# Each context group directly behind the scores of an even step, in a fused FFN, attention and FFN layer

## The chip, the core and the metric

The kernel runs on one core of a Trainium2 chip. Its time is the device time in microseconds (us) from launch to end; three runs of the kernel before took 852.42, 853.59 and 855.54 us, the median is 853.59 us. The core has TensorE (PE in the rows; PEld are its weight loads), VectorE (DVE), ScalarE (ACT), GpSimd (POOL) and SyncE (SP, which only issues DMAs here). Each engine works through its own instructions in order; they are held together by semaphores.

## The reference

The input x has 32 sequences of 256 tokens with 128 features (8192 tokens), float32. Three blocks follow one another:

```
x = x + 0.5 * ffn(layernorm(x))
x = x + attention(layernorm(x))
x = x + 0.5 * ffn(layernorm(x))

ffn(x):        h = concat([x, -x]);  h = 2*relu(s0 * h @ sign(k0));  h = 2*relu(s1 * h @ sign(k1))
               return s2 * h @ sign(k2)                 # 256 -> 512 -> 512 -> 128, weights +1 or -1
attention(x):  Q, K, V = x @ W.T + b, 16 heads of 8 features
               ctx = softmax(Q K^T / sqrt(8)) V         # per head, 256 x 256
               return layernorm(ctx + x) * gamma + beta
```

## The kernel before, in words

**Tiles and iterations.** A tile is 512 tokens, two sequences (b = 0, 1), so there are 16 tiles. `steps(it)` is written once for each engine and runs for iterations 0 to 16. An iteration has 32 steps (`UNITS`), and in it the stages of neighbouring tiles are interleaved by hand: the attention of tile t begins in step 0 of iteration t, its first FFN was done in the iteration before, the second half of its softmax falls into the first half of iteration t+1, and its second FFN later. Iterations 2 to 13 are the regular loop (`full`, L234). Iterations 0, 14 and 15 place the FFN pieces by tables of their own (`PACE_ZERO`, `PACE_FIRST`, `PACE_SECOND`, L44), iteration 1 has no FFN in its first half, and iteration 16 is the drain, with context places of its own (`AT_CONTEXT_LAST`).

**Attention.** 16 pairs p of a tile are two heads' scores for one sequence. In each even step `lanes` (L661) issues on TensorE the scores of pair s/2 into `ps_s` (L645) and, eight pairs behind, the shifted scores of another pair into `ps_t` (L658). VectorE takes row maxima of `ps_s` (`row_maxima`, L1049, the instruction of L1055). Scores wait until the maximum of the pair before is taken (`s_max`), shifted scores until the exponential of the pair before is taken (`s_exp`), since each has one buffer. ScalarE takes the exponential of `ps_t` into `probs` (`exps`, L824). The maxima of four pairs are split by GpSimd (L471 to L474), transposed by TensorE into the upper half of `ps_c` (`max_transpose`, L712, in steps 10, 17, 25 and 2), copied by ScalarE (`copy_max`, L833, in the step behind each: 11, 18, 26 and 3) and placed by a DMA as extra rows of Q, with which the shifted scores come out less their maximum.

**Context.** A context group is two pairs (four lanes): 16 float32 matmuls of 32 columns by 256 into the lower half of `ps_c` (`context`, L682, L698). There are eight groups a tile, C0 to C7. A group waits for the exponentials of its two pairs, and an even-numbered group (g % 2 == 0) also for the last copy out of `ps_c` (`c_free`) and for the maxima's copy (`mt_free`):

```
pe.wait_ge(s_exp, 2 * n + 2)
if g % 2 == 0:
    at_least(pe, c_free, GROUPS * t + grp // 2)
    ...
    pe.wait_ge(mt_free, 4 * t + (min(4, 2 + grp // 2) if last_tile else 2 + grp // 2))
```

Behind an odd-numbered group ScalarE copies the result to `ctx_t` (`context_copy`, L838, L841). Two of these, transposed by TensorE (`context_transpose`, steps 4 and 18, named CT0 and CT1), are divided by the softmax sums on VectorE and go to the tail on GpSimd (L477 to L499).

**FFN.** An FFN is 16 pieces (`ffn_piece`, L588). Piece 0 is the transpose of the normed input, pieces 2 to 5 the first layer (`ffn_in`, L560, L561), 6 to 11 the second (`ffn_mid`, L570, L571), 12 to 14 the last (`ffn_out`, L581, L583). Each result of 128 x 512 in one of the two banks `ps_z` is split in a high and a low float16 part: the high one by ScalarE (`z_split`, L798), then the low one by VectorE (`z_rest`, L1005, issued one step later), which frees the bank (`z_free`). In the regular loop the second FFN of a tile has pieces 2 to 14 in steps 2 to 14, the first FFN of a later tile in steps 18 to 30. Piece 0 stands in steps 15 and 31, and steps 0, 1, 16 and 17 have no FFN matmul.

**The order in a step.** On TensorE: `lanes` (in even steps), the context group if the step has one, the FFN piece, then the transposes and projections of the step (LNT 9, Q 12, K 15, V 31). On ScalarE: the exponentials, the FFN's split, the maxima's copy, the context's copy, the splits of the projections. On VectorE: the FFN rest of the step before, the row maxima, then norms, tail and projections.

Of the kernel before, what the change touches and what calls it, by code (L numbers as in the profile page):

```python
# [19 lines left out]
GROUPS, LANES = 4, 4  # L20
# [7 lines left out]
HALF = 16  # L28
# [59 lines left out]
def macaron_layer(nc, x, wq, bq, wk, bk, wv, bv, gamma, beta, k0, k1, k2, s0, s1, s2, out):  # L88
# [5 lines left out]
    with ExitStack() as ctx:  # L94
# [214 lines left out]
        def contexts(it, s):  # L309

            if not it.cur:
                return it.t - 1, 1 - it.par, (AT_CONTEXT_LAST.index(s) + 3,) if s in AT_CONTEXT_LAST else ()
            if s <= HALF + 1:
                return it.t - 1, 1 - it.par, (s // LANES + 3,) if it.prev and s % LANES == 1 else ()
            return it.t, it.par, ((s - HALF - 5) // LANES,) if s in (21, 25, 29) else ()

        def pair_of(p):

# [227 lines left out]
        def _(pe):  # L546
# [210 lines left out]
            def steps(it):  # L757
                t, par = it.t, it.par
                for s in range(UNITS):
                    lanes(it, s)  # L760
                    tile, parity, groups = contexts(it, s)
                    for g in groups:
                        context(tile, parity, g)
                    for f, _, piece in ffn_work(it, s):
                        ffn_piece(f, piece)
                    if it.prev:
                        if s == (AT_MAX[3] if it.cur else 1):
                            max_transpose(t - 1, 3)
                        for b in range(2):
                            if s == at(it, f"CT{b}"):  # L770
                                context_transpose(t - 1, b, it.misc[f"CT{b}"])
                    if it.cur:
                        for hb in range(3):
                            if s == AT_MAX[hb]:
                                max_transpose(t, hb)
                    if it.prep:
                        if s == at(it, "LNT"):
                            att_transpose(t + 1, 1 - par, it.misc["LNT"])
                        if s == at(it, "Q"):
                            project(0, it.misc["Q"])  # L780
                        if s == at(it, "K"):
                            project(1, it.misc["K"])
                        if s == at(it, "V"):
                            project_v(it.misc["V"])
# [7 lines left out]
        def _(act):  # L792
# [79 lines left out]
            def steps(it):  # L872
                t, par = it.t, it.par
                for s in range(UNITS):
                    tile, _, pairs = softmax_pairs(it, s)
                    for p in pairs:
                        exps(tile, p)
                    for f, _, piece in ffn_work(it, s):
                        ffn_piece(f, piece)

                    if it.prev and s - 1 == (AT_MAX[3] if it.cur else 1):
                        copy_max(t - 1, 3)
                    if it.cur and s - 1 in AT_MAX[:3]:
                        copy_max(t, AT_MAX.index(s - 1))
                    tile, _, groups = contexts(it, s)
                    for g in groups:
                        context_copy(tile, g)
                    if it.prep:
                        if s == at(it, "LNT"):
                            att_split(it.misc["LNT"])  # L890
                        if s == at(it, "Q"):
                            qk_split(0, it.misc["Q"])
                        if s == at(it, "K"):
                            qk_split(1, it.misc["K"])
                        if s == at(it, "V"):
                            v_copy(t + 1, 1 - par, it.misc["V"])
# [309 lines left out]
```

## Time and profile before

| | |
|---|---|
| median of three runs | 853.59 us |
| the profiled execution | 853.7 us |
| its span, first to last instruction | 851.9 us |
| TensorE busy, matmuls | 721.5 us (85%), 7258 matmuls |
| VectorE busy | 643.5 us (76%) |
| ScalarE busy | 513.3 us (60%) |
| GpSimd busy | 375.6 us (44%) |
| context matmuls (L698) | 2048, busy 139.6 us, idle before them 0.0 us |
| scores (L645) | 1024, busy 102.4 us, idle before them 39.0 us |
| row maxima (L1055) | 256, busy 312.4 us, 1220 ns each |
| mean granted clock of TensorE | 0.967 |

"Busy" is the time in which an engine has an instruction running; matmuls overlap in the pipeline, so a row's duration is longer than the distance to the next one. "Idle before" is the time in which an engine stood still just ahead of instructions of a row, with the instruction that ended it. A clock of 1.00 is TensorE's full speed, 2.4 GHz; 0.50 is 1.2 GHz.

### The profile page before, as it was taken

The numbers are of one execution on the slowest core, as the hardware profiler recorded it, in microseconds if no ns is written. First come the engines' busy times: TensorE is split into PE (matmuls) and PEld (weight loads), VectorE is DVE, ScalarE is ACT, GpSimd is POOL, SyncE is SP. The second block draws the span as 40 slices with busy tenths as digits, with TensorE's granted clock in tenths as the row PEclk, the third lists the DMA queues.
The fourth block names the chain that finished last, engine by engine and source line by source line (L and its number), as shares of the span: only waits on it lengthen the run. The fifth ranks groups of instructions, "written<-read, shape, count | busy, mean of one in ns | idle before, by whom it ended". The sixth has DMA issues, their size and how long they took to land. (4 is left out here: it accounts for less than half of the span.)

```text
span 851.9 us, 18411 instructions
## 1 busy us (share of the span) xinstructions
PE 721.5 (85%) x7258; PEld 325.4 (38%) x7258; DVE 643.5 (76%) x1228; ACT 513.3 (60%) x739; POOL 375.6 (44%) x663
## 2 busy tenths in 40 slices
PE   6768688899998988899998888899998987977666
PEld 2433234444443434444443334344443333332333
DVE  6558778878787888878787888878787887767343
ACT  3326566766666666766666666666666666656532
POOL 4522453536355353536355453536445453435240
PEclk9989899999999999999999999999999999989797
DMA  3101010101101010101101010100101010100000
GB/s 65 38 19 45 14 45 14 58 15 40 33 4 56 15 57 15 58 14 39 33 2 58 14 58 15 57 15 32 40 3 57 14 58 3 45 15 2 15 13 12
DMA packets 29508, 25.62 MB, mean 30 GB/s; under 512 B 4336, under 2 KB 29424, under 8 KB 29424
## 3 DMA queue, kind: packets, MB, share of 16 engines
q1 hardware_dynamic: 28992, 24.07, 9.1%
q8 instruction: 58, 0.95, 0.5%
q10 hardware_dynamic: 432, 0.39, 0.1%
q14 instruction: 26, 0.21, 0.1%
HBM read 5.05 MB, written 4.19 MB: 11 GB/s over the span
## 5 line engine op out<-in xcount | busy, mean ns | idle before, releaser
L1055 DVE TENSOR_REDUCE row_max<-ps_s 128x4 f32<-128x1024 f32 x256 | 312.4, 1220 | 89.8 <-PE ps_s L645 89.5
L830 ACT ACTIVATE probs<-ps_t,score_scale 128x1024 f32<-128x1024 f32 x256 | 283.9, 1109 | 122.8 <-PE ps_t L658 121.3
L798 ACT ACTIVATE ffn_hi<-ps_z 128x512 f16<-128x512 f32 x288 | 168.9, 592 | 139.0 <-PE ps_z L571 76.2
L1005 DVE SCALAR_TENSOR_TENSOR ffn_lo<-ps_z,ffn_hi 128x512 f16<-128x512 f32 x256 | 174.5, 686 | 74.8 <-ACT ffn_hi L798 71.9
L570 PE MATMUL ps_z<-ffn_hi,w 128*128 128x512 f16 x512 | 196.4, 384 | 5.9 <-DVE ffn_lo L1005 5.9
L571 PE MATMUL ps_z<-ffn_lo,w 128*128 128x512 f16 x512 | 194.9, 381 | 0.0
L698 PE MATMUL ps_c<-probs,v_cols 128*32 128x256 f32 x2048 | 139.6, 391 | 0.0
L645 PE MATMUL ps_s<-k_rows,q_rows 32*128 32x256 f16 x1024 | 102.4, 278 | 39.0 <-DVE row_max L1055 31.0
L658 PE MATMUL ps_t<-q_rows,k_rows 32*128 32x256 f16 x1024 | 102.2, 278 | 4.5 <-ACT probs L830 4.5
L471 POOL TENSOR_TENSOR max_scaled<-row_max,max_unit 128x16 f32<-128x16 f32 x64 | 14.2, 222 | 176.1 <-DVE row_max L1055 176.1
L570 PEld LDWEIGHTS ps_z<-ffn_hi,w 128*128 128x128 f16 x512 | 49.9, 98 | 88.4 <-issue 24.0
L698 PEld LDWEIGHTS ps_c<-probs,v_cols 128*32 128x32 f32 x2048 | 54.0, 110 | 61.3 <-issue 29.3
L645 PEld LDWEIGHTS ps_s<-k_rows,q_rows 32*128 32x128 f16 x1024 | 29.7, 92 | 123.8 <-DVE row_max L1055 87.8
L581 PE MATMUL ps_z<-w,ffn_hi 128*128 128x128 f16 x512 | 69.7, 224 | 3.9 <-DVE ffn_lo L1005 3.7
L560 PE MATMUL ps_z<-ffn_hi,w 128*128 128x512 f16 x128 | 51.6, 403 | 24.6 <-DVE ffn_lo L1005 20.2
L583 PE MATMUL ps_z<-w,ffn_lo 128*128 128x128 f16 x512 | 69.0, 223 | 0.0
L571 PEld LDWEIGHTS ps_z<-ffn_lo,w 128*128 128x128 f16 x512 | 50.3, 98 | 43.5 <-issue 1.0
L581 PEld LDWEIGHTS ps_z<-w,ffn_hi 128*128 128x128 f16 x512 | 48.8, 99 | 28.9 <-issue 20.4
L450 POOL TENSOR_TENSOR tail_ve<-tail_mv,eps 128x2 f32<-128x2 f32 x32 | 6.2, 195 | 114.5 <-DVE tail_mv L988 114.5
L583 PEld LDWEIGHTS ps_z<-w,ffn_lo 128*128 128x128 f16 x512 | 51.1, 100 | 0.3
L561 PE MATMUL ps_z<-ffn_lo,w 128*128 128x512 f16 x128 | 50.6, 395 | 0.0
L481 POOL TENSOR_TENSOR att_y<-ctx_n,xn_bv 128x256 f32<-128x256 f32 x32 | 23.3, 727 | 39.1 <-DVE ctx_n L1068 39.1
(119 smaller groups left out, 965.0 us busy)
## 6 DMA issues: line engine op xcount, KB each, us to landing
x<-L_attn_x SPq DMA_DIRECT2D x16, 256.0 KB, 2.7
q_rows<-q_hi SPq DMA_DIRECT2D x32, 128.0 KB, 2.1
y<-x SPq DMA_DIRECT2D x16, 256.0 KB, 2.1
k_rows<-k_hi SPq DMA_DIRECT2D x30, 128.0 KB, 2.1
q_rows<-q_lo SPq DMA_DIRECT2D x16, 128.0 KB, 2.1
q_rows<-no_max SPq DMA_DIRECT2D x16, 128.0 KB, 2.1
k_rows<-k_lo SPq DMA_DIRECT2D x15, 128.0 KB, 2.1
q_rows<-max_rows SPq DMA_DIRECT2D x64, 8.0 KB
```

The costliest lines, as they stand in the source:

```text
L560: pe.matmul(o[:], w0[:, m * P:(m + 1) * P], ffn_hi[:, 0, :], start=True, stop=False)
L570: pe.matmul(o[:], w, ffn_hi[:, 1 + k, :], start=(k == 0), stop=False)
L571: last = pe.matmul(o[:], w, ffn_lo[:, 1 + k, :], start=False, stop=(k == KC - 1))
L581: pe.matmul(o, ffn_hi[:, 5 + k, i * P:(i + 1) * P], w2[:, k, :], start=(i == 0 and k == 0), stop=False)
L583: last = pe.matmul(o, ffn_lo[:, 5 + k, i * P:(i + 1) * P], w2[:, k, :], start=False, stop=(i == TT - 1 and k == KC - 1))
L645: return pe.matmul(ps_s[:, i, a * SEQ:(a + 1) * SEQ], q_rows[par][r, g, c:c + P], k_rows[par][r, g, b * SEQ:(b + 1) * SEQ], start=True, st ...
L658: return pe.matmul(ps_t[:, i, a * SEQ:(a + 1) * SEQ], k_rows[par][r, g, c:c + P], q_rows[par][r, g, b * SEQ:(b + 1) * SEQ], start=True, st ...
L698: last = pe.matmul(ps_c[ROWS * j:ROWS * (j + 1), 0:SEQ], v[:, col:col + ROWS], probs[grp % 2][:, j, a * SEQ:(a + 1) * SEQ], start=(a == 0 ...
L798: a_.activation(ffn_hi[:, use, :], ps_z[use % 2][:], ACT.Relu if use else ACT.Copy, scale=1.0 if use else XN_SCALE).then_inc(z_hi, 1)
L830: a_.activation(probs[grp % 2][:, j:j + 2, :], ps_t[:], ACT.Exp, scale=score_scale[:, 0:1]).then_inc(s_exp, 1)
L1005: v.scalar_tensor_tensor(out=ffn_lo[:, use, :], in0=ps_z[use % 2][:], scalar=0.0, in1=ffn_hi[:, use, :], op0=ALU.max, op1=ALU.subtract).th ...
L1055: v.tensor_reduce(row_max[hb % 2][:].rearrange("p (a l) e -> p l a e", a=2)[:, j:j + 2, :, g % 2], ps_s[:].rearrange("p l (a k) -> p l a k ...
```

## The change

Only the helper `contexts(it, s)` is changed, which tells TensorE (matmuls) and ScalarE (copy) which context group stands in a step. In an iteration with current work the groups of the tile before stood in steps 1, 5, 9, 13 and 17 (C3 to C7) and those of the current tile in 21, 25 and 29 (C0 to C2). They now stand in steps 0, 4, 8, 12, 16 and 20, 24, 28. In these even steps the group comes directly behind `lanes` and ahead of the FFN piece and of the transposes and projections of the step. The drain (iteration 16) is as before, and so is every other instruction.

```diff
             if not it.cur:
                 return it.t - 1, 1 - it.par, (AT_CONTEXT_LAST.index(s) + 3,) if s in AT_CONTEXT_LAST else ()
-            if s <= HALF + 1:
-                return it.t - 1, 1 - it.par, (s // LANES + 3,) if it.prev and s % LANES == 1 else ()
-            return it.t, it.par, ((s - HALF - 5) // LANES,) if s in (21, 25, 29) else ()
+            if s <= HALF:
+                return it.t - 1, 1 - it.par, (s // LANES + 3,) if it.prev and s % LANES == 0 else ()
+            return it.t, it.par, ((s - HALF - LANES) // LANES,) if s in (20, 24, 28) else ()
```

`HALF` is 16, `LANES` is 4.

## Rows read from the trace of the kernel before

**Rows 1.** The header of the profile's page.
```profile
span 851.9 us, 18411 instructions
```

**Rows 2.** Windows: stretch and length; busy us (instructions) of PE, PEld, DVE, ACT, POOL; clock; DMA.
```profile
100.00:106.00 6.00, 4.42 (x30) 1.62 (x34) 3.62 (x7) 3.07 (x4) 4.26 (x6) 0.50 0.01 1
200.00:400.00 200.00, 180.74 (x1911) 82.40 (x1909) 164.78 (x312) 132.20 (x192) 96.07 (x171) 1.00 0.10 32
```

**Rows 3.** TensorE's timeline (start, duration, idle before): first scores of iterations 2 and 13.
```profile
134.41 0.28 PE L645 MATMUL ps_s<-k_rows,q_rows 32*128 32x256 f16 x2
...
662.81 0.28 PE L645 MATMUL ps_s<-k_rows,q_rows 32*128 32x256 f16 x2
```

**Rows 4.** TensorE's timeline, iteration 8, steps 4 to 8.
```profile
425.93 0.28 PE L645 MATMUL ps_s<-k_rows,q_rows 32*128 32x256 f16 x2
...
427.06 0.39 PE L560 MATMUL ps_z<-ffn_hi,w 128*128 128x512 f16 x1 [0.72 <-DVE ffn_lo L1005]
...
428.03 1.07 PE L698 MATMUL ps_c<-probs,v_cols 128*32 128x256 f32 x16
429.03 0.39 PE L560 MATMUL ps_z<-ffn_hi,w 128*128 128x512 f16 x1
...
432.18 0.28 PE L645 MATMUL ps_s<-k_rows,q_rows 32*128 32x256 f16 x2 [0.39 <-DVE row_max L1055]
```

**Rows 5.** ScalarE's timeline, iteration 8, steps 3 and 5.
```profile
426.64 0.36 ACT L836 ACTIVATE max_rows<-ps_c 16x256 f16<-16x256 f16 x1
...
429.67 0.60 ACT L798 ACTIVATE ffn_hi<-ps_z 128x512 f16<-128x512 f32 x1 [1.20 <-PE ps_z L561]
```

**Rows 6.** VectorE's timeline, iteration 8, steps 5 and 6.
```profile
428.64 0.68 DVE L1005 SCALAR_TENSOR_TENSOR ffn_lo<-ps_z,ffn_hi 128x512 f16<-128x512 f32 x1
...
430.30 0.69 DVE L1005 SCALAR_TENSOR_TENSOR ffn_lo<-ps_z,ffn_hi 128x512 f16<-128x512 f32 x1 [0.25 <-ACT ffn_hi L798]
430.91 1.22 DVE L1055 TENSOR_REDUCE row_max<-ps_s 128x4 f32<-128x1024 f32 x1
```

**Rows 7.** TensorE's timeline, iteration 8, steps 12 to 16.
```profile
440.36 0.28 PE L645 MATMUL ps_s<-k_rows,q_rows 32*128 32x256 f16 x2
...
440.69 0.23 PE L581 MATMUL ps_z<-w,ffn_hi 128*128 128x128 f16 x1
...
441.59 0.38 PE L619 MATMUL ps_m<-att_hi,wt_hi 128*128 128x512 f16 x1
...
442.55 1.07 PE L698 MATMUL ps_c<-probs,v_cols 128*32 128x256 f32 x16
...
444.11 0.28 PE L645 MATMUL ps_s<-k_rows,q_rows 32*128 32x256 f16 x2
...
446.30 0.28 PE L645 MATMUL ps_s<-k_rows,q_rows 32*128 32x256 f16 x2
```

**Rows 8.** ScalarE's timeline, iteration 8, steps 11 and 12.
```profile
440.96 0.36 ACT L836 ACTIVATE max_rows<-ps_c 16x256 f16<-16x256 f16 x1
...
442.66 0.69 ACT L815 ACTIVATE q_hi<-ps_m,b_fit 128x512 f16<-128x512 f32 x1 [0.34 <-PE ps_m L619]
```

**Rows 9.** VectorE's timeline, iteration 8, steps 13 and 14.
```profile
443.51 0.72 DVE L1046 SCALAR_TENSOR_TENSOR q_lo<-ps_m,b_fit,q_hi 128x512 f16<-128x512 f32 x1
444.54 1.23 DVE L1055 TENSOR_REDUCE row_max<-ps_s 128x4 f32<-128x1024 f32 x1 [0.31 <-PE ps_s L645]
```

**Rows 10.** TensorE's timeline, iteration 7, steps 17, 22 and 31.
```profile
400.44 0.28 PE L717 MATMUL ps_c<-ident,max_parts 128*16 128x128 f16 x2 [0.73 <-ACT ctx_t L841]
...
405.97 0.28 PE L645 MATMUL ps_s<-k_rows,q_rows 32*128 32x256 f16 x2 [0.31 <-DVE row_max L1055]
...
420.81 0.63 PE L554 MATMUL ps_z<-ident,ffn_xn 128*128 128x128 f32 x4 [0.30 <-POOL ffn_xn L455]
```

**Rows 11.** ScalarE's timeline, iteration 7, step 18.
```profile
402.62 0.36 ACT L836 ACTIVATE max_rows<-ps_c 16x256 f16<-16x256 f16 x1
```

**Rows 12.** VectorE's timeline, iteration 7, step 20.
```profile
404.69 1.22 DVE L1055 TENSOR_REDUCE row_max<-ps_s 128x4 f32<-128x1024 f32 x1
```

## The prediction, made before the change was run

> **What bounds the kernel now.** I read the page first, for the span and the share of each engine. Its header gives 851.9 us [rows 1]; the profiled execution took 853.7 us, so 1.8 us lie around the span. TensorE is the busiest engine with 85%, but it is no pure bound: in order, and interlocked with VectorE and ScalarE. Second I read the windows: in the middle of the run TensorE is busy 180.74 of 200 us at a granted clock of 1.00, which is 2.4 GHz [rows 2]. The reader is to see that its idle time is spread over the tiles, not gathered in one place. Third the timeline of one engine after the other for one tile. The scores of step 0 start at 134.41 us in tile 2 and at 662.81 us in tile 13 [rows 3]: 48.04 us a tile over 11 tiles, so one tile stands for the twelve of the regular loop. I write S4 for the scores of step 4, C4 for context group 4, and so on.
>
> In that tile no context matmul waits for anything: C4 starts at 428.03 behind a matmul, C6 at 442.55 [rows 4, 7]. TensorE waits elsewhere: 0.72 us for an FFN input [rows 4], 0.39 us for a row maximum at S8 [rows 4], and elsewhere for copies and norms [rows 10].
>
> **The change part by part.** Nothing is added or removed. Eight groups of 16 matmuls a tile move one step forward on TensorE, and ScalarE's copies of odd groups (L841) move with them. No DMA is moved, and no queue of SP or POOL is touched.
>
> *Edits that change nothing.* C3 (step 1 to 0) and C7 (17 to 16): in the regular loop no FFN piece stands in steps 0, 1, 16 or 17 ahead of the context, so TensorE's order stays. The odd groups' copies: ScalarE does the exps and the FFN copy of step 8 or 24 first, then L841, which is the order it has now. The copy of C5 and C1 now waits behind an FFN copy whose data comes later; its readers, the maxima's transposes of steps 10 and 25, stand behind three or more FFN products (1.3 us and more at some 0.43 us each, the distance of two L570 in the loop). I take 0, with 0.1 us a tile as the bad end.
>
> *The probabilities.* A context group needs the exps of its two pairs. The shifted scores of the same even step have already waited for the last of them (one buffer ps_t), so the early group finds them ready: cost 0.
>
> *The even groups' second wait, the core of it.* C4, C6, C0 and C2 also wait for ScalarE's copy of the maxima (mt_free, L693). That copy stands in ScalarE's steps 3, 11, 18 and 26, behind the FFN copy of its step. Today an FFN piece of one even step hides it. I take each in turn, in order of time.
>
> C4, step 4: S4 starts at 425.93 [rows 4], so C4 could start 0.33 us later (S12 to the next matmul, 440.36 to 440.69 [rows 7]), at 426.26. The maxima's copy ends at 426.64 + 0.36 = 427.00 [rows 5], and a waiter starts 0.06 us behind its releaser (the maximum of S20 ends at 404.69 + 1.22 = 405.91, S22 starts at 405.97 [rows 10, 12]): C4 at 427.06. By chance the FFN input L560 is released at 427.06 today [rows 4], so TensorE loses nothing: S6 stays. But that L560 is now behind C4, 1.00 us later (428.03 to 429.03 [rows 4]), at 428.06. Its ScalarE copy starts 0.64 us behind it and lasts 0.60 (429.03 to 429.67 [rows 4, 5]): ends 429.30. VectorE's rest (L1005) starts at 429.33 instead of 428.64 [rows 6], 0.69 late. From there to the row maximum of S6 it has 2.27 us today (428.64 to 430.91), in which it idles 0.25 us ahead of its next L1005 at 430.30 [rows 6]; an instruction that is not waited for starts 0.07 us ahead of the other's end, so 0.32 us of the delay is swallowed, and that maximum starts 0.37 late, at 431.28. S8 waits for just that maximum [rows 4]. **Term 1: +0.37 us.** The norm that follows on POOL hangs on the same VectorE chain and shifts alike.
>
> C6, step 12: S12 at 440.36 + 0.37 = 440.73, C6 possible at 441.06. The maxima's copy ends at 440.96 + 0.36 + 0.37 = 441.69 [rows 8]; C6 at 441.75. This wait of 0.69 us is new: today the FFN output (0.90 us) and the Q projection (0.96 us) stand there [rows 7]. Queued behind C6 are both of them, and all of TensorE. S12 to S14 was 3.75 us [rows 7] with the same work, now 4.44: S14 is 1.06 late. **Term 2: +0.69 us.**
>
> Is it given back before step 16? Q starts at 441.75 + 1.00 + 0.90 = 443.65; its copy 1.07 us later (441.59 to 442.66 [rows 7, 8]) and 0.69 long, to 445.41; VectorE's q_lo (0.72, row of 443.51 [rows 9]) runs 445.44 to 446.16, in front of the row maximum of S14, which would have started at 444.54 + 1.06 = 445.60 [rows 9] and now starts at 446.08 and ends at 447.31. S16 starts at 447.37 instead of 446.30 [rows 7]: 1.07 late. Nothing is given back, and VectorE has less slack left.
>
> Steps 16 to 31: the transposes of step 17 wait 0.73 us for the copy of C7 [rows 10]; that chain (S16, exps, copy) starts at S16, so it doesn't absorb a late S16. I add 0.04 us for VectorE's queue there: **1.1 us**. C0, step 20: released at 402.62 + 0.36 + 0.06 = 403.04 [rows 11], within the time in which TensorE would wait for the FFN; S22 waits for a row maximum that VectorE starts at 404.69 out of its own queue [rows 12], so 0. C2, step 28: it can fill a wait ahead of the FFN output, but at step 31 TensorE waits for POOL's FFN norm (0.30 us [rows 10]), whose chain doesn't move; what C2 wins, that wait grows by. 0.
>
> *Sum.* 12 tiles of the regular loop by 1.1 us are 13.2 us. Tiles 1, 14 and 15 have other FFN places and only part of the mechanism: between 0 and 1.1 us each, I take 0.6, 1.8 us together. Tile 0 and the drain: 0. So 853.7 + 13.2 + 1.8 = 868.7 us. The profiled execution is 0.1 us above the median of the runs (853.59), so the median should come out at 868.6, 1.8% slower.
>
> *A rule weighed.* Gaps of 0.3 to 0.7 us stand in each tile today [rows 4, 10], and the clock stays at 1.00 [rows 2]; by these rows one more gap of that size costs its own length and nothing else. The Trainium skill, "TensorE: Matmul & The Clock Gate", section "A second HAM failure mode: psum-queue depth-cycling", speaks against the change: frequent small idle gaps between groups of matmuls can make the clock swing between its two levels. By that rule the time would come out as in rival D, by the rows as in my sum.
>
> **The rivals.** A, faster: the contexts fill TensorE's waits for the FFN inputs. Place: step 4 with its 0.72 us [rows 4], and step 20, which has the same order of work. If VectorE had room and the maxima's copies were early, S6 and S22 would come earlier by this, 1.44 us a tile, 12 tiles 17 us: 836 us. It decides where S22 is released by something other than the row maximum. Against it: S22 and S8 wait for that engine now [rows 4, 10], and C4 is itself released at 427.06.
>
> B, no change: the 1.07 us at S16 is absorbed by the 0.73 us wait of step 17. That leaves 0.34 by 12 = 4.1 us, with half of the outer tiles' 1.8 us 5 us: 859 us; only if also term 1 vanishes, 854 us. Against it: the chain of that wait starts at S16.
>
> C, slower still: the late q_lo pushes VectorE's queue: the row maximum of S14 starts 1.54 us late (444.54 to 446.08). If the maximum of S16, behind it in the queue, and S18 take this over in full, 18.5 us + 1.8: 874 us. For it: VectorE runs maximum, residual, rest and maximum without a gap there. Against: step 17 has a wait of its own, for the copy of C7 [rows 10], which is only 1.07 late.
>
> D, the clock: the stretch of 100 to 106 us has 0.50 granted, which is 1.2 GHz [rows 2]. If the new gaps brought such a stretch of 6 us to each tile, its matmuls would take twice as long, some 3 us a tile: 868.7 + 36 = 905 us. Against it: the largest new gap, 0.69 us, is no longer than the 0.72 us of today.
>
> **How the numbers follow.** Chances: forecast 0.76, C 0.08, B 0.08 (half of it within 0.5% of before), A 0.06, D 0.02. The predicted time is 868.7. The terms' own error is some 0.3 us a tile, 4 us; downward, term 2 alone (12 by 0.69) gives 862; upward C gives 874. The range is 860 to 877. About 0.5%, or 4.3 us, is what a measurement of this kernel can tell from no change: faster than that 0.05, within it 0.06, slower 0.89.
>
> **What would show it.** In the timeline of the changed kernel: C4 starts at once with the end of the maxima's copy, a gap ahead of C6 of some 0.7 us put down to ScalarE's copy L836, no gap at C0 that moves S22; S4 to S8 grows by 0.37 us and S12 to S14 by 0.7; a tile takes 49.1 us where it took 48.0; S16 to S0 of the next tile is unchanged; TensorE's idle time grows by as much as the span, the busy time of no engine changes; the clock stays at 1.00 in the loop. Wrong would be: context groups with no wait ahead of them (then ScalarE's copies come earlier than I place them, and A or B holds), or a growth that sits in steps 16 to 31.

## The result and the profile after

The changed kernel took 877.35 us (median of 4 runs, 871.51 to 878.70) beside 854.34 us for the kernel before: ratio 1.0258, 95% interval 1.0207 to 1.0310. Run again it took 872.29 us (5 runs, 871.86 to 873.94) beside 855.86 us (17 runs): ratio 1.0201, interval 1.0187 to 1.0215. The second comparison has the narrower interval; how far the spread of the first can be explained is told below. The forecast was 868.6 us for the median (868.7 for the profiled execution), a ratio of 1.0176. The profiled execution took 871.5 us, with a span of 869.7 us: 17.8 us more than before [rows 1], where the working had 15.0.

The page of the changed kernel: the header, the share of TensorE, and the group of the context matmuls (busy us, mean ns, then idle us before them with what ended it).

```profile
span 869.7 us, 18411 instructions
...
PE 717.2 (82%) x7258; PEld 329.7 (38%) x7258; DVE 642.4 (74%) x1228; ACT 513.1 (59%) x739; POOL 375.3 (43%) x663
...
L698 PE MATMUL ps_c<-probs,v_cols 128*32 128x256 f32 x2048 | 141.1, 394 | 22.8 <-ACT max_rows L836 22.6
```

The reader is to see the last line. Before, the context matmuls never waited; now TensorE stands still for 22.8 us just ahead of them, nearly all of it for ScalarE's copy of the maxima (L836). Not all of this is lost: before, part of the same time was a wait for FFN inputs (TensorE idle ahead of the products of L560: 24.6 us before, 8.6 us now).

The window against the second of [rows 2]. In the loop the clock is 1.00 as before; TensorE is busy 175.21 of 200 us instead of 180.74.

```profile
200.00:400.00 200.00, 175.21 (x1831) 81.31 (x1831) 159.58 (x303) 128.51 (x187) 94.11 (x164) 1.00 0.10 31
```

TensorE's timeline, first scores of tiles 2 and 13, as in [rows 3]: (677.96 - 135.55) / 11 = 49.31 us a tile, before 48.04.

```profile
135.55 0.28 PE L645 MATMUL ps_s<-k_rows,q_rows 32*128 32x256 f16 x2
...
677.96 0.28 PE L645 MATMUL ps_s<-k_rows,q_rows 32*128 32x256 f16 x2
```

TensorE, iteration 8, steps 4 to 8, against [rows 4]:

```profile
434.73 0.28 PE L645 MATMUL ps_s<-k_rows,q_rows 32*128 32x256 f16 x2
...
435.94 1.07 PE L698 MATMUL ps_c<-probs,v_cols 128*32 128x256 f32 x16 [0.81 <-ACT max_rows L836]
436.94 0.39 PE L560 MATMUL ps_z<-ffn_hi,w 128*128 128x512 f16 x1
...
438.35 0.28 PE L645 MATMUL ps_s<-k_rows,q_rows 32*128 32x256 f16 x2
...
441.42 0.28 PE L645 MATMUL ps_s<-k_rows,q_rows 32*128 32x256 f16 x2 [0.53 <-DVE row_max L1055]
```

ScalarE and VectorE in the same steps, against [rows 5] and [rows 6]:

```profile
435.44 0.36 ACT L836 ACTIVATE max_rows<-ps_c 16x256 f16<-16x256 f16 x1
...
437.58 0.60 ACT L798 ACTIVATE ffn_hi<-ps_z 128x512 f16<-128x512 f32 x1 [0.79 <-PE ps_z L561]
```

```profile
438.21 0.69 DVE L1005 SCALAR_TENSOR_TENSOR ffn_lo<-ps_z,ffn_hi 128x512 f16<-128x512 f32 x1 [0.69 <-ACT ffn_hi L798]
...
439.55 0.68 DVE L1005 SCALAR_TENSOR_TENSOR ffn_lo<-ps_z,ffn_hi 128x512 f16<-128x512 f32 x1
440.14 1.22 DVE L1055 TENSOR_REDUCE row_max<-ps_s 128x4 f32<-128x1024 f32 x1
```

C4 waits for the copy; S6 comes 3.62 us after S4 (before 3.64), so nothing is lost there. The FFN input is now behind C4, VectorE stands idle 0.69 us for it, and the row maximum that S8 waits for is late. S4 to S8 takes 6.69 us instead of 6.25.

TensorE, ScalarE and VectorE in steps 11 to 16 of iteration 8, against [rows 7], [rows 8] and [rows 9]:

```profile
449.60 0.28 PE L645 MATMUL ps_s<-k_rows,q_rows 32*128 32x256 f16 x2
...
450.69 1.07 PE L698 MATMUL ps_c<-probs,v_cols 128*32 128x256 f32 x16 [0.70 <-ACT max_rows L836]
...
452.60 0.38 PE L619 MATMUL ps_m<-att_hi,wt_hi 128*128 128x512 f16 x1
...
454.01 0.28 PE L645 MATMUL ps_s<-k_rows,q_rows 32*128 32x256 f16 x2
...
456.33 0.28 PE L645 MATMUL ps_s<-k_rows,q_rows 32*128 32x256 f16 x2
```

```profile
450.19 0.36 ACT L836 ACTIVATE max_rows<-ps_c 16x256 f16<-16x256 f16 x1
...
453.67 0.69 ACT L815 ACTIVATE q_hi<-ps_m,b_fit 128x512 f16<-128x512 f32 x1 [2.12 <-PE ps_m L619]
```

```profile
454.39 0.75 DVE L1046 SCALAR_TENSOR_TENSOR q_lo<-ps_m,b_fit,q_hi 128x512 f16<-128x512 f32 x1 [1.56 <-ACT q_hi L815]
455.05 1.22 DVE L1055 TENSOR_REDUCE row_max<-ps_s 128x4 f32<-128x1024 f32 x1
```

The wait ahead of C6 is 0.70 us; S12 to S14 takes 4.41 us, before 3.75. Then q_lo stands in front of the row maximum of S14, and S16 follows 2.32 us after S14, before 2.19. At the other end of the tile, iteration 7 against the last row of [rows 10]: the transpose of step 31 waits 0.76 us for POOL, before 0.30.

```profile
429.60 0.63 PE L554 MATMUL ps_z<-ident,ffn_xn 128*128 128x128 f32 x4 [0.76 <-POOL ffn_xn L455]
```

### The profile page after: what moved, and what is told of

The parts are those of the page before. It is cut to its first block and busy times, and to the rows that moved or that the text cites. A ratio compares the mean times of both kernels' runs of the same rounds, so it can differ in the third digit from the quotient of the medians.

```text
span 869.7 us, 18411 instructions
## 1 busy us (share of the span) xinstructions
PE 717.2 (82%) x7258; PEld 329.7 (38%) x7258; DVE 642.4 (74%) x1228; ACT 513.1 (59%) x739; POOL 375.3 (43%) x663
## 5 line engine op out<-in xcount | busy, mean ns | idle before, releaser
L698 PE MATMUL ps_c<-probs,v_cols 128*32 128x256 f32 x2048 | 141.1, 394 | 22.8 <-ACT max_rows L836 22.6
L698 PEld LDWEIGHTS ps_c<-probs,v_cols 128*32 128x32 f32 x2048 | 57.7, 111 | 74.2 <-issue 54.6
L581 PE MATMUL ps_z<-w,ffn_hi 128*128 128x128 f16 x512 | 67.5, 223 | 0.2
L583 PE MATMUL ps_z<-w,ffn_lo 128*128 128x128 f16 x512 | 66.9, 222 | 0.0
L560 PE MATMUL ps_z<-ffn_hi,w 128*128 128x512 f16 x128 | 51.3, 401 | 8.6 <-DVE ffn_lo L1008 5.0
```

The costliest lines, as they stand in the source:

```text
L560: pe.matmul(o[:], w0[:, m * P:(m + 1) * P], ffn_hi[:, 0, :], start=True, stop=False)
L581: pe.matmul(o, ffn_hi[:, 5 + k, i * P:(i + 1) * P], w2[:, k, :], start=(i == 0 and k == 0), stop=False)
L583: last = pe.matmul(o, ffn_lo[:, 5 + k, i * P:(i + 1) * P], w2[:, k, :], start=False, stop=(i == TT - 1 and k == KC - 1))
L698: last = pe.matmul(ps_c[ROWS * j:ROWS * (j + 1), 0:SEQ], v[:, col:col + ROWS], probs[grp % 2][:, j, a * SEQ:(a + 1) * SEQ], start=(a == 0 ...
```

## The experiments

The theory (W in the expectations): a tile grows by two things, the new wait of TensorE ahead of C6 for the copy of the maxima, with the late Q behind it, and the FFN input delayed behind C4, which reaches S8 through VectorE. The rivals: any context group ahead of an FFN piece costs (F); the two costs share one slack, so that taking one away gives back little (B, not the B of the prediction); the clock (K, the prediction's D).

All runs in one table. The distances are medians over tiles 2 to 13 of each profile, from the starts of the scores in TensorE's timeline; the ratio is against the kernel before, run beside it.

| kernel | median us | ratio, 95% interval | tile | S4-S8 | S12-S14 | S14-S16 | S28-S30 | S30-S0 |
|---|---|---|---|---|---|---|---|---|
| before | 855.9 | 1 | 47.98 | 6.25 | 3.74 | 2.19 | 3.23 | 2.71 |
| changed, again | 872.29 | 1.0201 (1.0187-1.0215) | 49.27 | 6.69 | 4.41 | 2.32 | 2.78 | 3.17 |
| odd groups only | 855.65 | 1.0010 (0.9996-1.0024) | 47.99 | 6.25 | 3.75 | 2.19 | 3.24 | 2.71 |
| C6 back | 862.59 | 1.0082 (1.0069-1.0095) | 48.43 | 6.69 | 3.74 | 2.19 | 2.78 | 3.17 |
| C4 back | 865.55 | 1.0120 (1.0088-1.0151) | 48.81 | 6.25 | 4.41 | 2.32 | 2.78 | 3.17 |
| maxima's copy first | 862.24 | 1.0075 (1.0060-1.0090) | 48.27 | 6.21 | 3.64 | 2.32 | 2.78 | 3.17 |
| behind the piece | 856.89 | 1.0018 (1.0008-1.0028) | 48.20 | 6.30 | 3.74 | 2.32 | 3.23 | 2.71 |
| C0, C1, C2 only | 855.44 | 0.9996 (0.9985-1.0006) | 47.97 | 6.25 | 3.74 | 2.19 | 2.77 | 3.17 |
| C2 and early norm | 843.74 | 0.9861 (0.9845-0.9878) | 47.03 | 6.25 | 3.74 | 2.19 | 2.78 | 2.22 |
| early norm alone | 843.48 | 0.9850 (0.9827-0.9873) | 47.13 | 6.25 | 3.74 | 2.19 | 2.88 | 2.22 |

**The changed kernel again.** No edit.

> The changed kernel again, unaltered. Its first profile had a span of 869.7 us at a mean granted clock of 0.970, but three other executions took 876.4 to 878.7 us at a clock of 0.955 to 0.962. Theory W (the cost is the wait of the even context groups for the copy of the maxima, and the late FFN input behind C4): a regular tile takes 49.25 us again, the loop is at clock 1.00, and the spread of 7 us sits outside the regular loop, in the tiles around 100 us and behind 720 us, where the clock already falls. Theory K (the new gaps bring the clock down in the loop): some regular tiles take longer than 49.3 us, with a granted clock under 1.00 in their windows, and these make up the spread. Median 871 to 879 us by both; a profile at a clock under 0.965 would decide.

The tile is 49.27 us, the clock in the loop 1.00. So K falls for the loop. Its profile had a mean clock of 0.968, so it says little on the spread between runs; the next kernel's profile says more.

**Odd groups only.**

```diff
-            if s <= HALF:
-                ... if it.prev and s % LANES == 0 else ()
-            return ..., ((s - HALF - LANES) // LANES,) if s in (20, 24, 28) else ()
+            if s <= HALF + 1:
+                ... if it.prev and s in (0, 5, 8, 13, 16) else ()
+            return ..., ((s - HALF - LANES) // LANES,) if s in (21, 24, 29) else ()
```

> Only the odd groups stand in even steps (C3 0, C5 8, C7 16, C1 24); C4, C6, C0 and C2 are back in 5, 13, 21 and 29. Theory W: odd groups have no wait for the maxima's copy, so a regular tile takes 47.97 us as before, at most 0.1 us more, and the time is that of before, 852 to 856 us. Theory F (it is the delay of the FFN pieces by a context group ahead of them that costs, whichever group it is): half of the extra 1.28 us a tile is here, 48.6 us a tile, 861 to 863 us.

A tile takes 47.99 us and the time is that of before: F falls. C5 and C1 ahead of the FFN products cost nothing. In step 8 ScalarE's copy of such a product starts 3.27 us behind S8 instead of 2.27, but VectorE's rest starts 4.08 us behind S8 where it started 4.07: until then VectorE is busy with its row maximum and a norm. The group's place costs only where something that is waited for is late by it.

This profile had a long span (859.1 us at a mean clock of 0.958) with the loop of the kernel before: from tile 2 to tile 14 it takes 576.52 us (before 576.37), up to tile 2 it takes 2.4 us more and from tile 14 on 4.7 us more. Ahead of the first scores of tile 0, where the edit changes nothing, it takes 52.69 us at a granted clock of 0.87, before 50.45 us at 0.93; from tile 14 to the end the clock is 0.86, before 0.89. Windows of this kernel, and TensorE's context group in step 13 of tile 14:

```profile
200.00:400.00 200.00, 180.11 (x1902) 83.29 (x1902) 164.31 (x311) 131.18 (x192) 96.36 (x168) 1.00 0.10 31
728.00:736.00 8.00, 7.62 (x51) 2.10 (x48) 6.26 (x10) 4.96 (x8) 3.23 (x6) 0.69 0.00 1
```

```profile
726.38 1.08 PE L610 MATMUL ps_m<-ident,att_xn 128*128 128x128 f32 x4 [3.36 <-POOL att_xn L455]
...
731.74 1.67 PE L698 MATMUL ps_c<-probs,v_cols 128*32 128x256 f32 x16
...
733.34 0.39 PE L570 MATMUL ps_z<-ffn_hi,w 128*128 128x512 f16 x1
```

The same groups of the kernel before, with a window that starts as far behind L610 as the one above, 1.6 us (the row of 200 to 400 us is in [rows 2]):

```profile
725.47:733.47 8.00, 7.57 (x63) 2.38 (x66) 6.93 (x11) 6.13 (x8) 3.53 (x7) 0.87 0.01 3
```

```profile
723.85 0.78 PE L610 MATMUL ps_m<-ident,att_xn 128*128 128x128 f32 x4 [3.35 <-POOL att_xn L455]
...
728.30 1.07 PE L698 MATMUL ps_c<-probs,v_cols 128*32 128x256 f32 x16
...
729.30 0.39 PE L570 MATMUL ps_z<-ffn_hi,w 128*128 128x512 f16 x1
```

In tile 14 TensorE waits 3.35 us for POOL's norm in both, and is then granted about half the clock: 0.57 from 724 to 728 us in the kernel before, 0.51 from 726 to 732 us here. In one execution it was back at full speed by the context group (16 matmuls in 1.07 us), in the other not yet (1.67 us). In the 8 us of the windows it was granted 0.87 of the clock in the one and 0.69 in the other, and from L610 to the FFN product behind the context group it took 5.45 us (723.85 to 729.30) and 6.96 us (726.38 to 733.34): 1.5 us for this one place. So between these two executions the difference is in the outer tiles, not in the loop.

Whether the 876 to 879 us of the first comparison have this cause too is not shown. None of those three runs left a trace, and the mean clock alone does not give their time: at 0.962 a run took 876.38 us there and 873.19 us in the second comparison.

**C6 back in step 13.**

```diff
-                ... if it.prev and s % LANES == 0 else ()
+                ... if it.prev and s in (0, 4, 8, 13, 16) else ()
```

> The changed kernel with C6 alone back in step 13. Theory W: the 0.70 us wait ahead of C6 goes, and with it the late Q projection; left are 0.46 us from C4 and 0.05 us: a regular tile takes 48.4 to 48.5 us, S12 to S14 3.75 us again, the profiled span is 859 to 861 us. Theory B (C4 and C6 share one slack, so that taking one away gives back little): a tile stays above 48.9 us.

**C4 back in step 5.** The same line with `s in (0, 5, 8, 12, 16)`.

> The changed kernel with C4 alone back in step 5; C6 stays in 12. Theory W: the late FFN input behind C4 goes (S4 to S8 6.25 us again instead of 6.69), the wait ahead of C6 stays (S12 to S14 4.4 us), and the late q_lo with it: a regular tile takes 48.8 us, the profiled span is 864 to 866 us. With the run that has C6 back (48.43 us) the two parts then add up to the whole of 1.28 us. Theory B (shared slack): the parts don't add up, a tile is at 49.1 us or more.

TensorE, first with C6 back (S12, C6 and S14), then with C4 back (S8, S12 and C6):

```profile
396.49 0.28 PE L645 MATMUL ps_s<-k_rows,q_rows 32*128 32x256 f16 x2
...
398.68 1.07 PE L698 MATMUL ps_c<-probs,v_cols 128*32 128x256 f32 x16
...
400.24 0.28 PE L645 MATMUL ps_s<-k_rows,q_rows 32*128 32x256 f16 x2
```

```profile
242.70 0.28 PE L645 MATMUL ps_s<-k_rows,q_rows 32*128 32x256 f16 x2 [0.39 <-DVE row_max L1055]
...
250.88 0.28 PE L645 MATMUL ps_s<-k_rows,q_rows 32*128 32x256 f16 x2
...
251.97 1.07 PE L698 MATMUL ps_c<-probs,v_cols 128*32 128x256 f32 x16 [0.70 <-ACT max_rows L836]
```

With C6 back the 0.70 us wait is gone and S14 is 3.75 us behind S12; with C4 back S8 waits 0.39 us again, as before [rows 4], and C6's wait is untouched. Taking C6 back gives 49.27 - 48.43 = 0.84 us, taking C4 back 0.46 us: together 1.30, the whole change 1.29. The two parts add up, so B falls, and both expected tile times were met to 0.03 us.

**The maxima's copy first.** On ScalarE, in each step:

```diff
-                    for f, _, piece in ffn_work(it, s):
-                        ffn_piece(f, piece)
                     if it.prev and s - 1 == (AT_MAX[3] if it.cur else 1):
                         copy_max(t - 1, 3)
                     if it.cur and s - 1 in AT_MAX[:3]:
                         copy_max(t, AT_MAX.index(s - 1))
+                    for f, _, piece in ffn_work(it, s):
+                        ffn_piece(f, piece)
```

> The changed kernel, but ScalarE copies the maxima ahead of the FFN split of its step instead of behind it (steps 3, 11, 18, 26); no other engine's order is changed, so all context groups stay early. Theory W: C6 no longer waits, C4 is released some 0.4 us earlier, S6 and S8 are where they were before; a regular tile takes 48.0 to 48.2 us and the time is 853 to 858 us, near the kernel before. Theory F: the FFN pieces are still delayed by the context groups, a tile stays at 49.0 us or more and the time at 868 us or more.

TensorE, S12, C6 and S14:

```profile
396.25 0.28 PE L645 MATMUL ps_s<-k_rows,q_rows 32*128 32x256 f16 x2
...
396.58 1.07 PE L698 MATMUL ps_c<-probs,v_cols 128*32 128x256 f32 x16
...
399.89 0.28 PE L645 MATMUL ps_s<-k_rows,q_rows 32*128 32x256 f16 x2
```

C6 starts 0.33 us behind S12 without a wait, although it stands in the same early place: the 0.7 us need both, the early group and a copy that stands behind the FFN split; taking away either one ends them. S4 to S8 is down too (6.21 us). A tile takes 48.27 us, a little over the expected 48.2, because the copy now delays the FFN split of step 18: VectorE's rest behind it starts 0.24 us later against S18 (2.35 instead of 2.11 us), and S20 to S22 takes 3.77 us (before 3.58), which I had not expected. The time, 862.2 us, is 4 us above what I had expected. Of the span's 9.0 us more than before, 12 by 0.29 = 3.5 us are the loop; the rest lies before tile 2 (2.4 us, of which 1.1 us ahead of tile 0, where the edit changes nothing) and behind tile 13 (3.1 us), and what part of it is the order there and what part the clock stays open.

**Behind the piece.** On TensorE, in each step (the drain shares these lines and changes with them):

```diff
-                    for g in groups:
-                        context(tile, parity, g)
                     for f, _, piece in ffn_work(it, s):
                         ffn_piece(f, piece)
+                    for g in groups:
+                        context(tile, parity, g)
```

> The changed kernel, but on TensorE the context group stands behind the FFN piece of its even step instead of ahead of it, still ahead of the transposes and projections (C4 behind the FFN input and ahead of CT0, C6 behind the FFN output and ahead of Q). All groups stay in their even steps (the drain, which shares this line, is changed with it). Theory W: the piece covers the maxima's copy, so no context group waits for it, and no FFN input is delayed behind C4; what is left is Q, late by one context group (1.0 us), of which a late row maximum of S14 may take up to 0.1 us: a regular tile takes 47.97 to 48.1 us, time 855 to 858 us. If the late Q alone were the price in steps 12 to 16, S12 to S16 would stay at 6.7 us (before 5.94) and a tile at 48.7 us, 865 us.

TensorE (S12, C6, Q, S14) and VectorE behind it:

```profile
393.65 0.28 PE L645 MATMUL ps_s<-k_rows,q_rows 32*128 32x256 f16 x2
...
394.97 1.07 PE L698 MATMUL ps_c<-probs,v_cols 128*32 128x256 f32 x16
395.98 0.39 PE L619 MATMUL ps_m<-att_hi,wt_hi 128*128 128x512 f16 x1
...
397.39 0.28 PE L645 MATMUL ps_s<-k_rows,q_rows 32*128 32x256 f16 x2
```

```profile
397.77 0.75 DVE L1046 SCALAR_TENSOR_TENSOR q_lo<-ps_m,b_fit,q_hi 128x512 f16<-128x512 f32 x1 [0.89 <-ACT q_hi L815]
398.44 1.22 DVE L1055 TENSOR_REDUCE row_max<-ps_s 128x4 f32<-128x1024 f32 x1
```

With the FFN output as cover C6 waits for nothing, S12 to S14 is 3.74 us as before, and Q is late by one group all the same. That is the price of the late Q by itself: q_lo ahead of the row maximum, 0.13 us from S14 to S16, and with steps 4 to 8 (0.05) and 16 to 22 (0.05) 0.22 us a tile, 0.1 more than the end of my expectation.

**Only C0, C1 and C2 moved.** The kernel before with `((s - HALF - LANES) // LANES,) if s in (20, 24, 28)` in its last line.

> The kernel before with only C0, C1 and C2 moved (20, 24, 28); C3 to C7 stay in 1, 5, 9, 13, 17. Theory W: a regular tile takes 47.97 us as before: S20 to S22 unchanged (VectorE), S28 to S30 0.45 us shorter, S30 to the next S0 0.45 us longer, because the transpose of step 31 waits for POOL's norm. Time 852 to 857 us. Rival A in its small form (what C2 wins is kept): 47.5 us a tile, 848 us.

TensorE, S30, the transpose of step 31 and the next S0:

```profile
226.90 0.28 PE L645 MATMUL ps_s<-k_rows,q_rows 32*128 32x256 f16 x2
...
228.61 0.63 PE L554 MATMUL ps_z<-ident,ffn_xn 128*128 128x128 f32 x4 [0.76 <-POOL ffn_xn L455]
...
230.06 0.28 PE L645 MATMUL ps_s<-k_rows,q_rows 32*128 32x256 f16 x2
```

S30 comes 0.46 us earlier and S0 0.46 us later behind it: what C2 wins, the wait for POOL takes (0.76 us here, 0.30 before [rows 10]). This is the small form of rival A, and it is worth 0.

**C2 moved and an earlier norm; the earlier norm alone.** Both start from the kernel before; the first also has C2 in step 28.

```diff
-AT_STATS_PREP, AT_STATS_B, AT_STATS_A = 6, 7, 26
+AT_STATS_PREP, AT_STATS_B, AT_STATS_A = 6, 7, 25
```

> The kernel before with C2 alone moved (29 to 28) and VectorE's statistics for the next FFN norm (AT_STATS_A) in step 25 instead of 26, so that POOL's norm starts some 1.6 us earlier. Theory W: the wait ahead of the transpose in step 31 goes, 0.4 us for itself and 0.45 us that C2 wins: 47.1 us a regular tile, time 842 to 846 us. If something behind step 31 takes the place (the exps of step 0, the maxima's transposes), 47.5 to 47.97 us and 848 to 854 us.

> The kernel before with AT_STATS_A = 25 alone. Theory W: only the 0.3 to 0.4 us of waiting in step 31 goes: 47.6 us a regular tile, time 848 to 850 us, so that the move of C2 is worth 0.45 us a tile by the difference to the run that has both. If the move of C2 is worth nothing even then, both runs have the same time.

The earlier norm alone, TensorE in steps 30 to 0, then VectorE in steps 25 to 28:

```profile
416.27 0.28 PE L645 MATMUL ps_s<-k_rows,q_rows 32*128 32x256 f16 x2
...
417.05 0.61 PE L554 MATMUL ps_z<-ident,ffn_xn 128*128 128x128 f32 x4
...
418.49 0.28 PE L645 MATMUL ps_s<-k_rows,q_rows 32*128 32x256 f16 x2
```

```profile
409.82 0.87 DVE L982 BATCH_NORM_STATS2 ffn_bn<-x 128x6 f32<-128x128 f32 x4 [0.36 <-POOL x L492]
411.32 1.23 DVE L1055 TENSOR_REDUCE row_max<-ps_s 128x4 f32<-128x1024 f32 x1 [0.63 <-PE ps_s L645]
412.46 0.37 DVE L988 BATCH_NORM_AGGREGATE ffn_mv<-ffn_bn 128x2 f32<-128x6 f32 x4
412.90 0.69 DVE L1005 SCALAR_TENSOR_TENSOR ffn_lo<-ps_z,ffn_hi 128x512 f16<-128x512 f32 x1
```

The transpose of step 31 waits for nothing. I had expected 47.6 us a tile and 848 to 850 us; it is 47.13 us and 843.5, a miss. The statistics no longer stand between the row maximum of S26 and the FFN rest that the output products of step 28 need, so the wait of TensorE in step 28 goes as well (S28 to S30 2.88 us, before 3.23). For the same reason C2's move is worth only 0.10 us a tile on top (47.03), and not the 0.45 us that I gave it: the wait that it was to fill had gone. That the kernel with both came out as expected (47.03 us for 47.1, 843.7 us for 842 to 846) is therefore luck: the two parts were wrongly shared out. Both kernels beat the kernel before by 1.4 to 1.5%; by their intervals they can't be told apart.

## Why the prediction was right

**The order of the edits.** C3, C7 and the odd groups at 0: right (odd groups only, 47.99 us a tile). The exps: no context matmul waits for them in the loop.

**Term 1, C4.** Right in its mechanism, each link seen: C4 just behind the end of the copy, S6 unmoved, VectorE idle for the delayed FFN input, S8 behind its row maximum. Forecast 0.37, measured 0.44 us (6.69 - 6.25), and 0.46 us a tile when it is taken back. The difference is the size of one input: I took 0.06 us from a releaser's end to the waiter's start, from VectorE's maximum to S22. From the end of ScalarE's copy to C4 it is 435.94 - (435.44 + 0.36) = 0.14 us, and for C6 450.69 - (450.19 + 0.36) = 0.14 us too.

**Term 2, C6.** Forecast 0.69 us, the wait is 0.70; S12 to S14 grew by 0.67 us. The late q_lo ahead of the row maximum of S14 came as worked out, and with the 0.08 us of the release twice in the chain S16 is 1.23 us late instead of 1.07. "Nothing is given back" was right, and the prediction's rival B with it wrong.

**Steps 16 to 31.** Forecast 0.04 us, measured 0.05. C0 waits, but S22 does not move; C2's gain of 0.45 us is the growth of the wait for POOL, shown by the run with C0, C1 and C2 alone. So rival A fell as argued, and C too: S16 to S18 grew by 0.05 us only.

**The sum.** A tile was to grow by 1.1 us and grew by 1.27 to 1.29. Twelve tiles: 13.2 forecast, 15.3 measured (the loop from tile 2 to tile 14 is 591.66 us long, before 576.37). The outer tiles: 1.8 forecast, 17.8 - 15.3 = 2.5. That these are near each other is in part luck. The working had 0.6 us each in tiles 1, 14 and 15 and nothing elsewhere; the two profiles differ by 0.38 us ahead of tile 0, where the change does nothing, by 0.46 in tile 0, 0.30 in tile 1 and 1.44 in tile 14, and by -0.07 from tile 15 on. How much of this is the order and how much the clock is not shown.

The two medians were 2.0 and 2.6% slower instead of 1.8. The first, 877.35 us, lies 0.35 us above the range of 860 to 877 us as written; measured by the ratio to the kernel before it is inside (1.0258, where 877 to 853.59 is 1.0274). My range had no term for the spread from run to run, which was 871.51 to 878.70 us there, and what made it is open.

**The rule on small gaps.** With gaps of up to 0.81 us in each tile, and one of 1.05 us in iteration 8, the clock stayed at 1.00 from 140 to 690 us in the changed kernel; it did so in every variant of it too, and rival D fell. The Trainium skill, "TensorE: Matmul & The Clock Gate", section "A second HAM failure mode: psum-queue depth-cycling", describes a swing that no loop of this case shows. "The busy time of no engine changes" missed slightly: TensorE's fell from 721.5 to 717.2 us.

## What to carry to other kernels

A group of work that "has its data" early may still carry a second wait, for a buffer or a copy by another engine; before moving it forward on an in-order engine, lay the end of each of its releasers beside its new start. What stands between two waits is cover: the same groups behind the FFN piece cost 0.2 us a tile, ahead of it 1.3 us. And a move pays only up to the next wait that has another origin: C2's 0.45 us went to the wait for POOL, and the cheap edit was to feed that norm earlier, which by itself made the kernel 1.5% faster.

## What was not expected of the hardware

The time from the end of a releasing instruction to the start of the waiting matmul was 0.14 us from ScalarE's copy of the maxima to a context group and 0.06 us from VectorE's row maximum to scores. Why they differ was not tried. After nearly the same wait (3.35 and 3.36 us) in tile 14 TensorE was back at full clock before its context group in one execution and not in the other.
